# One program, three stages: the fourth sequence's attention of layer 0 placed after the experts, and a dispatch without slot copies

## The reference, cut to what matters

```python
x = L0_attn_x
xn = _layernorm(x, axis=-1)
x = x + _L0_attn_ref(xn, Wq, Wk, Wv) + _L0_ffn_ref(xn, Wr, br, W1, b1, W2, b2)
xn = _layernorm(x, axis=-1)
x = x + _L1_attn_ref(xn, W_qkv, W_out) + _L1_ffn_ref(xn, W_r, W_k, W_v, mu_r, mu_k)
return x
```

## Time and profile before

| what | us |
|---|---|
| median of 3 runs (lowest to highest) | 975.34 (974.9 to 976.41) |
| the profiled execution, its own time | 976.55 |
| its span, first to last instruction | 974.8 |
| TensorE busy | 904.5 (93%) |
| VectorE busy | 744.7 (76%) |
| ScalarE busy | 583.1 (60%) |
| GpSimd busy | 196.6 (20%) |
| mean granted TensorE clock, share of full speed | 0.972 |

### The profile page before, as it was taken

One profiled execution on the slowest core, in us unless ns is written; L12 is line 12 of the kernel. 1 busy time (PEld: TensorE's weight loads), 2 busy tenths in 40 slices (PEclk: granted clock), 3 DMA queues, 4 the chain that ended last, 5 costly groups with the idle time before them and its releaser, 6 DMA issues. The chain is left out here.

```text
span 974.8 us, 19161 instructions
## 1 busy us (share of the span) xinstructions
PE 904.5 (93%) x6533; PEld 843.1 (86%) x6533; DVE 744.7 (76%) x1440; ACT 583.1 (60%) x1139; POOL 196.6 (20%) x240
## 2 busy tenths in 40 slices
PE   3899999989999999999999999999386799899998
PEld 2688999989999999999999999999274787778877
DVE  7676555558888888888888888888378578697764
ACT  3643434436666666666666666666275458486581
POOL 1004666500000000000000000000552045163202
PEclk9899999999999999999999999999797899999999
DMA  8791333509766666666666666662321022031101
GB/s 264 263 296 60 114 116 116 191 13 379 246 216 215 215 215 215 215 215 215 218 215 222 223 222 224 222 220 73 81 71 38 11 65 66 1 92 37 44 0 44
DMA packets 103813, 150.36 MB, mean 154 GB/s; under 512 B 8480, under 2 KB 86880, under 8 KB 103648
## 3 DMA queue, kind: packets, MB, share of 16 engines
q1 hardware_dynamic: 94592, 123.13, 38.6%
q0 software_dynamic: 9184, 26.75, 7.9%
HBM read 112.63 MB, written 37.22 MB: 154 GB/s over the span
## 5 line engine op out<-in xcount | busy, mean ns | idle before, releaser
L956 ACT ACTIVATE h<-ps,b1T 128x256 f32<-128x256 f32 x312 | 129.7, 467 | 139.6 <-PE ps L891 139.3
L889 PE MATMUL ps<-w2h,hh 128*128 128x256 f32 x624 | 179.6, 288 | 0.3 <-DVE hl L1010 0.3
L889 PE MATMUL ps<-xTh,w1h 128*128 128x256 f32 x624 | 177.4, 284 | 1.4 <-DVE xTl L993 1.4
L890 PE MATMUL ps<-xTl,w1h 128*128 128x256 f32 x624 | 177.3, 284 | 0.0
L891 PE MATMUL ps<-xTh,w1l 128*128 128x256 f32 x624 | 177.2, 284 | 0.0
L891 PE MATMUL ps<-w2h,hl 128*128 128x256 f32 x624 | 176.8, 283 | 0.0
L890 PE MATMUL ps<-w2l,hh 128*128 128x256 f32 x624 | 176.6, 283 | 0.0
L1010 DVE TENSOR_TENSOR hl<-h,hh 128x512 fp32r<-128x512 f32 x156 | 107.7, 691 | 52.2 <-ACT hh L960 50.6
L889 PEld LDWEIGHTS ps<-xTh,w1h 128*128 128x128 f32 x624 | 120.5, 193 | 1.6 <-DVE xTl L993 1.6
L891 PEld LDWEIGHTS ps<-xTh,w1l 128*128 128x128 f32 x624 | 120.6, 193 | 0.0
L890 PEld LDWEIGHTS ps<-xTl,w1h 128*128 128x128 f32 x624 | 120.5, 193 | 0.0
(11 more groups left out here) (230 smaller groups left out, 2138.6 us busy)
## 6 DMA issues: line engine op xcount, KB each, us to landing
raw<-in_L_ffn_W SPq DMA_DIRECT2D x40, 1024.0 KB
raw_odd<-in_L_ffn_W SPq DMA_DIRECT2D x38, 1024.0 KB, 8.4
dispatched<-shared SPq DMA_DIRECT2D x1, 9984.0 KB, 34.9
rows<-dispatched SPq DMA_DIRECT2D x39, 256.0 KB, 6.1
expert_out<-y POOLq DMA_DIRECT2D x38, 256.0 KB, 6.9
xn_rows<-raw SPq DMA_DIRECT2D x4, 1024.0 KB, 5.3
rows<-xn_rows SPq DMA_DIRECT2D x32, 128.0 KB
x_acc<-in_L_attn_x SPq DMA_DIRECT2D x3, 1024.0 KB, 8.9
```

The source lines that it names most:

```text
L889: pe.matmul(out, ah, bh, start=start, stop=False, skip_group_check=True)
L890: pe.matmul(out, ah, bl, start=False, stop=False, skip_group_check=True)
L956: op = act.activation(h32[:, k, :], ps[:, q, (k % 2) * M:(k % 2 + 1) * M], ACT.Relu, bias=s.b1T[:, ds(e * HC + k, 1)])
```

## The change

- **Layer 0.** `attend` runs for three sequences (0 to 2), of which the third now has `last` set, so nothing is prepared in it for a fourth. The normalised, turned rows of sequence 3 stay in `xnT_last`, and the folded weights in `folded`; both are now held through the experts.
- **Dispatch.** The slot copy is gone; the scatter's offsets are read from `s.slots`, and the tiles are written out instead of looped.
- **Third block.** It begins with the fourth sequence's attention (`attend_last`), all eight projections included. Beside it: the 16 gathers of layer 1's first sequence on GpSimd, that sequence's two `combine` units of four tiles and `scales` on VectorE, its square roots, normalisation and copies on ScalarE, and its transposes (`turn(0, 0)`, `turn(0, 1)`) on TensorE. The split of `W_qkv` also moves into the attention.
- **Layer 1.** All sequences now have two units of four tiles; the special order of the first body is gone. The first products of the first body wait for all of the attention (`attended`).
- `xn`, `xl` and `prob` of the third block lie in other buffers than before (`xnT_last`, `folded`, `qk`).

The diff, cut to its core:

```diff
         def sequences(eng, body):
-            for b in range(B):
-                body(b, b == 0, b == B - 1)
+            for b in range(B - 1):
+                body(b, b == 0, b == B - 2)
...
-            for u in range(4):
-                load_rows(u, u)
-            with sp.Fori(1, NT // 4) as g:
-                for u in range(4):
-                    sp.wait_ge(scattered[u], 16 * K * g)
-                    load_rows(4 * g + u, u)
+            for t in range(NT):
+                if t >= 4:
+                    sp.wait_ge(scattered[t % 4], 16 * K * (t // 4))
+                load_rows(t, t % 4)
...
-                pool.tensor_copy(slot_now[:, u, :], s.slots[:, ds(K * t, K)]).then_inc(slot_staged, 1)
-                hold(pool, slot_staged, t + 1, passed)
-                hold(pool, row_loaded[u], 16 if turn is None else 16 * turn + 16, passed)
+            for t in range(NT):
+                pool.wait_ge(row_loaded[t % 4], 16 * (t // 4) + 16)
                 for k in range(K):
-                    pool.indirect_dma_start(out=dispatched, out_offset=bass.IndirectOffsetOnAxis(
-                        ap=slot_now[:, u, k:k + 1], axis=0), in_=xrow[:, u], in_offset=None).then_inc(scattered[u], 16)
+                    slot = s.slots[:, K * t + k:K * t + k + 1]
+                    pool.indirect_dma_start(out=dispatched, out_offset=bass.IndirectOffsetOnAxis(ap=slot, axis=0),
+                                            in_=xrow[:, t % 4], in_offset=None).then_inc(scattered[t % 4], 16)
...
         def units(b):
-            if isinstance(b, int) and b == 0:
-                return [(2 * u, 2, u + 1) for u in range(4)]
-            return [(4 * h, 4, 2 * b + h + 3) for h in range(2)]
+            return [(4 * h, 4, 2 * b + h + 1) for h in range(2)]
...
+            beside_attention = [(proj_mm, PROJECTED + n) for n in (1, 3, 5)]
+            beside_attention += [(score_mm, ATTENDED + a) for a in (1, 2, 3, 4)]
...
+            def attend_last():
+
+                project(range(NPROJ - 1))
+                scores(0)
+                for a in range(BT):
+                    if a + 1 < BT:
+                        scores(a + 1)
+                    turn_rows(a)
+                    if a == 0:
+                        pe.wait_ge(attended, ATTENDED + 2)
+                        project([NPROJ - 1])
+                    if 0 < a < BT - 1:
+                        values(a - 1)
+                    if a == 5:
+                        turn(0, 0)
+                    if a == 6:
+                        pe.wait_ge(xnT_ready, 2)
+                        turn(0, 1)
+                values(BT - 2)
+                values(BT - 1)
+
             def body(b, first, last):
...
+                    if first and n < 2:
+                        pe.wait_ge(attended, ATTENDED + BT + 2)
...
+            softmax(0)
+            for a in range(BT):
+                if a + 1 < BT:
+                    softmax(a + 1)
+                turned_hi(a)
+                if a == 0:
+                    project_hi([NPROJ - 1])
+                    act.wait_ge(s.later_loaded, 16 * 4)
+                    act.activation(wqkvh[:, :, :], s.wqkv, ACT.Copy).then_inc(wh_ready, 1)
+                if a == 2:
+                    deviation(0, 0)
+                if a == 3:
+                    normalized(0, 0)
+                    deviation(0, 1)
+                if a == 4:
+                    normalized(0, 1)
+                if a == 5:
+                    act.wait_ge(const_ready, 3)
+                    turned_out(0, 0)
+                if a == 6:
+                    turned_out(0, 1)
...
+            for a in range(BT):
+                if a + 1 < BT:
+                    row_max(a + 1)
+                rows_lo(a)
+                if a == 0:
+                    project_lo([NPROJ - 1])
+                    dve.wait_ge(wh_ready, 1)
+                    V.tensor_tensor(wqkvl[:, :, :], s.wqkv, wqkvh[:, :, :].bitcast(F32), ALU.subtract
+                                    ).then_inc(wl_ready, 1)
+                if 0 < a < BT - 1:
+                    add_attention(a - 1)
+                if a == 1:
+                    combine(0, 0)
+                if a == 2:
+                    scales(0, 0)
+                    combine(0, 1)
+                if a == 3:
+                    scales(0, 1)
+                if a == 6:
+                    turned_lo(0, 0)
+            add_attention(BT - 2)
+            add_attention(BT - 1)
             turned_lo(0, 1)
```

More of the change, by code:

```diff
@@ L1157, in gather_beside @@
                         gather(pool, s, expert_out, b + 1, i)
-            for i in range(BT // 2):
-                gather(pool, s, expert_out, 0, i)
+            gather(pool, s, expert_out, 0, 0)
             pool.memset(same_head[:, :], 1.0).then_inc(const_ready, 1)
@@ new lines, in scores @@
+            def scores(a):
+                i = ORDER[a]
+                if a < 2:
+                    pe.wait_ge(proj_lo, PROJECTED + NZ + 1 + 2 * a)
+                L = (i + 1) * P
+                for h in range((L + 511) // 512):
+                    w = min(512, L - 512 * h)
+                    bank, ks = ps[:, 2 * (a % 2) + h, 0:w], slice(512 * h, 512 * h + w)
+                    for c in range(DC):
+                        three(bank, zh[:, c, tile_of(i)], zl[:, c, tile_of(i)], kh[:, c, ks], kl[:, c, ks],
+                              c == 0, False)
+                pe.matmul(bank[:, w - P:w], s.ident_b[:, :], s.above[:, :], start=False, stop=True,
+                          skip_group_check=True).then_inc(score_mm, 1)
@@ new lines, in turn_rows @@
+            def turn_rows(a):
+                pe.wait_ge(prob_ready, ATTENDED + a + 1)
+                if a == 0:
+                    pe.wait_ge(weights_ready, 1)
+                if a > 0:
+                    pe.wait_ge(pT_lo, ATTENDED + a)
+                for j in range(ORDER[a] + 1):
+                    mm = pe.transpose(ps[:, 4 + j // 4, (j % 4) * P:(j % 4 + 1) * P], prob[:, a % 2, tile_of(j)],
+                                      s.ident[:, :])
+                mm.then_inc(prob_turned, 1)
@@ new lines, in values @@
+            def values(a):
+                i = ORDER[a]
+                pe.wait_ge(pT_lo, ATTENDED + a + 1)
+                if a == 0:
+                    pe.wait_ge(proj_lo, PROJECTED + NPROJ)
+                pe.wait_ge(attended, ATTENDED + a + 1)
+                for j in range(i + 1):
+                    mm = three(ps[:, 6 + a % 2, 0:D], pTh[:, a % 2, j], pTl[:, a % 2, j], vh[:, j, :], vl[:, j, :],
+                               j == 0, j == i)
+                mm.then_inc(pv_mm, 1)
+            def attend_last():
[17 more added lines that the diff above has]
+                values(BT - 1)
@@ L1456, in body @@
                 if not last:
-                    normed(b + 1, 0)
-                    if not first:
-                        normed(b + 1, 1)
+                    for u in range(2):
+                        deviation(b + 1, u)
+                        normalized(b + 1, u)
                 for m in range(4):
                     h, c = m // 2, m % 2
-                    if first and m == 2:
-                        normed(b + 1, 1)
                     act.wait_ge(att_turned, 4 * b + m + 1)
@@ new lines, in add_attention @@
+            def add_attention(a):
+                i = ORDER[a]
+                V.reciprocal(row_inv[:, i:i + 1], row_sum[:, i:i + 1]).then_inc(inv_done, 1)
+                dve.wait_ge(inv_done, ATTENDED + a + 1)
+                dve.wait_ge(pv_mm, ATTENDED + a + 1)
+                V.scalar_tensor_tensor(x_tile(LAST * BT + i), ps[:, 6 + a % 2, 0:D], row_inv[:, i:i + 1],
+                                       x_tile(LAST * BT + i), ALU.mult, ALU.add).then_inc(attended, 1)
+            for half in range(2):
+                at = slice(half * 512, (half + 1) * 512)
+                dve.wait_ge(kh_ready, LAST + half + 1)
+                V.tensor_tensor(kl[:, :, at], s.xnT_last[:, :, at], kh[:, :, at].bitcast(F32), ALU.subtract
+                                ).then_inc(kl_ready, 1)
@@ L1611, in body @@
                     scales(b + 1, 0)
-                    if not first:
-                        combine(b + 1, 1)
+                    combine(b + 1, 1)
                 apply_gate(0)
                 apply_gate(1)
-                if not last and not first:
+                if not last:
                     scales(b + 1, 1)
@@ L1619, in body @@
                 divide(1)
-                if first:
-                    combine(b + 1, 1)
-                    scales(b + 1, 1)
                 apply_gate(2)
```

234 lines of the change are left out of this document (145 added, 89 removed).

## The result

The changed kernel takes 959.4 us (median of 4 runs, 958.9 to 962.1) where the kernel before takes 975.5: ratio 0.984, 95% interval 0.982 to 0.986. The profiled execution took 959.39 us, its span is 957.7.

| step, us | predicted | measured |
|---|---|---|
| experts' first transposes | 173.7 (-42.2) | 174.20 (-41.7) |
| third block's first transposes | 647.3 | 648.21 |
| from there to the first body's first product | 64.2 | 64.23 |
| first body | 61.2 | 59.49 |
| from the second body to the end | 184.0 | 185.77 |

A forecast was written before the change was run, and what follows sets the result against it. TensorE was taken as full in layer 0 and the experts, with 17 + 21.5 us of room after them. Front -42.2, start to first body +47.3, first body -23.2: -18.1 us, hence 957.5 us; 8-in-10 range 949 to 967.

The forecast's parts named there:

- Front: Before the experts: one attention fewer and a dispatch hidden behind the third start the experts 42.2 us earlier, at 173.7.
- the rows are there at 168.2, 5.5 us before they are wanted: Dispatch's end: scatters every 1.27 us end at 163.5, then 1.55 us to the row load, 0.4 issue, 2.7 landing.
- Moved attention: Third block's start to first body's first product: transposes 2.8, projections 10.1, clock 1.0, attention 34.1, insertions 16.2; 64.2 us.
- low clock on the path: Rival, moved attention: TensorE's slow stretches after three idle stretches aren't covered, 3 x 2.3 = 6.9 us; 964 us, 18%.
- First body: Layer 1's first body takes the second's form: 62.85 us less 1.6 gives 61.2 us, bounds 59.5 and 62.9.
- every instruction stays: From the second body's first product, at 772.7 against 790.78 (18 us earlier), to the end, nothing changes.
- The dispatch that keeps its pace: Rival, layer 0's dispatch: scatters stay at 1.71 us, experts start at 195.6 instead of 173.7; 979 us, 7%.
- The insertions can be hidden: Rival, moved attention: VectorE's inserted pieces fall into its idle time, 16.2 us become 1.8; 943 us, 12%.
- Double table cost: Rival, ScalarE's table switches: a second 1.28 us behind two loads on the path, 2.6 us; 960 us, 5%.
- The lock of VectorE on GpSimd's descriptors: Dispatch: VectorE's two-port mode blocks GpSimd's descriptor writes; hardly seen in the trace, but would give 979 us.

The follow-up runs named there:

- the repeats: The changed kernel run again without edit, twice: 958.8 us (ratio 0.983 to the kernel before), and 959.4 us (0.982) on a third chip.
- Early split: Changed kernel with layer 1's weight split moved from between the moved attention's second and third row maximum to among its projections: 958.0 us, ratio 0.982.
- thin combine: Changed kernel with 6 of the 8 additions left out of each of the moved attention's two combines: 954.0 us, ratio 0.977.
- no-roots run: Changed kernel with the moved attention's two square roots replaced by a copy of their operand (wrong numbers there): 958.7 us, ratio 0.982.

## Why the prediction was right

- *Front, -42.2: right in size (-41.7), wrong in its margin.* The step "the rows are there at 168.2, 5.5 us before they are wanted" failed. The landing of the last scatter was taken as 1.55 us from a row where the weights' loads had been issued 9.1 us ahead of its end and were nearly through; now they are issued 7.1 us ahead, and it was 4.35. The prediction saw the weights move forward, but not that they would meet the last scatter. From the row load's issue to the transposes 3.1 us were taken; issue and landing are as predicted (0.4 and 2.6 or 2.7), but the transposes follow 5.76 us after the issue, and for the other 2.7 the prediction has no term. Together 5.5 us: the margin is 0.2 or none, and the dispatch begins to cost at 1.29 us per scatter, not at 1.36. That the forecast held is luck: the scatters came every 1.29 us, with nothing to spare.
- *Moved attention, 64.2: right in its middle, and in its sum (64.23, in the repeats 63.8 and 63.2) by two misses that cancel.* Third maximum +1.8 (predicted 1.8), fourth +4.2 (4.4), fifth +5.1 (5.2), sixth +2.1 (2.1): from first to sixth 34.75 us for 35.0. Early split (1.80 for 1.8) and thin combine (4.64 of 4.74) confirm the mechanism. The two ends missed:

  | us | predicted | first profile | repeats |
  |---|---|---|---|
  | block's start to first maximum | 16.9 | 15.3 | 16.1, 15.5 |
  | first to sixth maximum | 35.0 | 34.75 | 34.8, 34.8 |
  | sixth maximum to the first body | 12.3 | 14.2 | 12.9, 12.9 |

  In the first profile the weight transposes took 1.5 us at full clock instead of 2.8, and no projection ran at the low clock, for which 1.0 us stood in the sum. TensorE idles 4.5 and 3.3 us ahead of the transposes of steps 3 and 4, and the low clock was rightly costed at nothing there. But it came again behind the 2.7 us of idle time at step 5: granted 0.50 from 701 to 704 us, the last two maxima 4.5 us apart instead of the 3.2 of the repeats, where it was 1.00 in the same stretch. These 1.3 us were on the path: a part of the rival *low clock on the path*.
- *First body, 61.2: too high by 1.7 us in the profile*, 59.5 being the lower bound given; five of the eleven profiles with the moved attention have 59.5 or 59.6, the others 61.0 to 62.9, by where the low clock falls.
- *From the second body on "every instruction stays": the instructions do, the clock doesn't.* The third body took 63.5 against 61.5 us, 2.0 more, of which the prediction had nothing; in the third profile it took 61.8. So the total of 958.5 for 959.39 rests on chance too: 1.7 us too much for the first body and 1.8 us too little for what follows.
- *Rivals.* The dispatch that keeps its pace was sized 195.6 and 979 us; with the old dispatch it is 195.5 and 981. The 195.5 agree by luck: the last scatter ended 2.7 us earlier than before (188.2 for 190.95), and the 2.7 us missing behind the row load made it up. The rival was wrongly argued in one point: the idle 0.9 us were neither the copy's nor GpSimd's own. Without the two `hold` 0.28 us are left behind the same copy. The insertions can be hidden (949.6), but only in another order. Double table cost: each table load lasts 1.28 us, with the next instruction 0.01 us behind it:

```profile
685.04 1.28 ACT L1480 ACT_TABLE_LOAD   x1
686.33 0.30 ACT L1480 ACTIVATE std<-mv,eps 128x4 f32<-128x4 f32 x1
686.64 1.28 ACT L1517 ACT_TABLE_LOAD   x1
```

The Trainium skill (ScalarE: Activation LUTs, "What ACT_TABLE_LOAD costs") adds a drain of about 1.38 us to each; no row here shows it, and the no-roots run agrees with the 1.28.

- *The lock of VectorE on GpSimd's descriptors* (the Trainium skill, SBUF — State Buffer, "SBUF: two separate sides"): hardly seen. Beside a busy VectorE two of the 64 scatters of the changed kernel take 1.4 and 1.7 us instead of 0.96, some 1.2 us in all, and whether that is the lock no run shows. What was seen on one chip is the opposite: GpSimd kept its pace (1.27 us, no scatter over 1.2), and the others stood.

## What to carry to other kernels

Place side work behind the instruction that others wait for, in pieces no longer than the idle time there: the same combines, scales and split made this block 12 us longer, and the kernel 9 us slower, ahead of the maxima than behind them. A margin that rests on a landing time must take it from a row with the same traffic at the same distance beside it, and count from the first issue to the first use, with everything in between. Before trusting a long run of GpSimd scatters without pauses beside busy engines, time it on more than one chip.

## What the runs showed of the hardware

- Behind the last indirect scatter of 128 rows of 1 KB the load that waits for it is issued after 1.53 us with no load beside it, after 1.55 where two loads of 1 MB were issued 9.1 us ahead of the scatter's end, after 2.50 at 8.0 us and after 4.3 to 4.7 at 7.1.
- Scatters of GpSimd come every 1.27 to 1.29 us without anything between; a copy and its semaphore add 0.18 us per pair, two `hold` behind it 0.63 us more.
- On one of three chips, 64 such scatters in a row left TensorE 49 of some 490 products in 70 us in both profiles of them (mean granted clock 0.56), and ten runs of ten took 77 us longer; the cause is open.
- Equal bodies differ by 2 us between profiles through stretches at lower granted clock (0.97 against 1.00), and their sum can hide it (within 0.2 us in three profiles of the changed kernel) or not (244.9 to 247.5 over eleven profiles with the moved attention).
